# Gathering a token's two expert rows one per attention head over 64 heads, instead of two per head over the first 32

## What is computed

```python
# attention: two softmax maps for each head, and their difference
a1 = softmax(q1 @ k1.T * scale) @ v;  a2 = softmax(q2 @ k2.T * scale) @ v
o = rms_norm(a1 - lam * a2, sub_norm_w) * (1 - LAMBDA_INIT)
attn = o @ w_proj.T + b_proj
# experts: each token has two slots f1, f2 in the experts' rows eo, and two gates
eo = gelu(disp @ w_gate) @ w_down                     # (8 experts x 1024 slots, 256)
ffn = (g1 * keep1)[:, None] * eo[f1] + (g2 * keep2)[:, None] * eo[f2]
out = x + attn + ffn
```

## Time and profile before

| | |
|---|---|
| runs | 1810.17, 1812.2, 1918.32 us |
| profiled execution | 1807.14 us, span 1805.3 us |
| mean granted TensorE clock | 0.991 of full speed |
| TensorE busy | 1722.3 us (95%) |
| VectorE busy | 1486.1 us (82%) |
| ScalarE busy | 1402.3 us (78%) |
| GpSimd busy | 578.0 us (32%) |
| indirect gathers of expert rows | 64, 64.4 us on GpSimd, mean 1006 ns |

### The profile page before, as it was taken

How to read it: one execution, slowest core, us unless ns; L and a number is a source line. 1 busy time by engine, 2 the same in 40 slices (tenths; PEclk the granted TensorE clock), 3 DMA queues, 4 the chain that set the end, 5 groups by cost and what they waited for, 6 DMA issues and landing times.

```text
span 1805.3 us, 39337 instructions
## 1 busy us (share of the span) xinstructions
PE 1722.3 (95%) x15555; PEld 749.3 (42%) x15555; DVE 1486.1 (82%) x1727; ACT 1402.3 (78%) x2639; POOL 578.0 (32%) x1065
## 2 busy tenths in 40 slices
PE   6869999999999999999999999999999999999998
PEld 5437888888885222222222222222222222222226
DVE  7767777777767899898998999999999999999913
ACT  4535454445435999999999999999999999999993
POOL 1474221222200345445454454532121211112140
PEclk9989999999999999999999999999999999999999
DMA  7564233122203111111111111110101010100002
GB/s 239 197 216 148 93 108 94 59 71 88 89 12 117 35 44 36 49 34 40 45 37 48 35 41 43 38 41 23 32 23 32 23 29 27 27 11 5 5 1 94
DMA packets 92280, 109.66 MB, mean 61 GB/s; under 512 B 17472, under 2 KB 67264, under 8 KB 92096
## 3 DMA queue, kind: packets, MB, share of 16 engines
q1 hardware_dynamic: 85952, 90.36, 16.0%
q0 software_dynamic: 6144, 16.79, 3.2%
HBM read 72.77 MB, written 33.82 MB: 59 GB/s over the span
## 4 chain that ended last, share of the span: by engine, by line
PE 66%; ACT 27%; POOL 3%; DVE 2%; issue 1%; DMA 1%; ACTq 0%; SPq 0%; DVEq 0%; POOLq 0%
ACT arena_t L780 25%; PE banks L1223 18%; PE banks L1211 12%; PE banks L1262 10%; PE banks L1242 10%; PE banks L1193 8%; POOL arena_v L558 2%; PE banks L1282 2%; ACT o_raw L759 2%; PE banks L1116 2%; PE banks L1344 2%; PE banks L1162 1%; PE banks L1127 0%; DMA arena_x<-x_in 0%; DVE row_half L993 0%
## 5 line engine op out<-in xcount | busy, mean ns | idle before, releaser
L993 DVE TENSOR_REDUCE row_half<-banks 128x2 f32<-128x1024 f32 x1024 | 1189.7, 1218 | 144.7 <-PE banks L1193 136.5
L780 ACT ACTIVATE arena_t<-banks 128x512 f32<-128x512 f32 x2048 | 1085.2, 600 | 57.7 <-PE banks L1211 30.9
L1223 PE MATMUL banks<-arena_t,v_ring 128*17 128x256 f32 x8192 | 643.6, 386 | 26.2 <-ACT o_raw L759 26.1
L1223 PEld LDWEIGHTS banks<-arena_t,v_ring 128*17 128x17 f32 x8192 | 136.2, 95 | 403.4 <-issue 244.2
L1211 PE MATMUL banks<-arena_q 50*128 50x512 bf16 x960 | 286.2, 383 | 0.6 <-ACT arena_t L780 0.3
L1211 PE MATMUL banks<-qk_ring 50*128 50x512 bf16 x896 | 267.1, 387 | 7.1 <-ACT arena_t L780 4.1
L1193 PE MATMUL banks<-arena_q 48*128 48x512 bf16 x960 | 268.4, 384 | 0.5 <-DVE row_half L993 0.2
L1193 PE MATMUL banks<-qk_ring 48*128 48x512 bf16 x896 | 249.1, 382 | 1.1 <-DVEq L986 1.0
L744 ACT ACTIVATE arena_t<-banks 128x512 f32<-128x512 f32 x128 | 76.5, 598 | 205.8 <-PE banks L1242 197.1
L1262 PE MATMUL banks<-w_parts,hidden_parts 128*128 128x256 f32 x1536 | 196.3, 286 | 0.0
L1262 PEld LDWEIGHTS banks<-w_parts,hidden_parts 128*128 128x128 f32 x1536 | 187.1, 192 | 13.6 <-issue 13.6
(11 more groups left out here) (147 smaller groups left out, 1355.0 us busy)
## 6 DMA issues: line engine op xcount, KB each, us to landing
expert_rows<-arena_r SPq DMA_DIRECT2D x16, 512.0 KB, 3.0
q_stack<-arena_q SPq DMA_DIRECT2D x8, 768.0 KB, 4.9
k_stack<-arena_q SPq DMA_DIRECT2D x8, 768.0 KB, 3.5
v_heads<-arena_v SPq DMA_DIRECT2D x4, 1088.0 KB, 5.6
v_ring<-v_heads SPq DMA_DIRECT2D x64, 68.0 KB, 3.0
arena_x<-x_in SPq DMA_DIRECT2D x4, 1024.0 KB, 6.3
token_rows<-arena_x SPq DMA_DIRECT2D x4, 1024.0 KB, 7.8
arena_v<-w_gate_in SPq DMA_DIRECT2D x4, 1024.0 KB, 6.7
```

Of the source, the lines that this page charges most:

```text
L780: nc.scalar.activation(probs[:, kt % PSLOTS, q, :], banks[:, ST_BANKS[ring_place(i) % 3], :], ACT.Exp).then_inc(exp_done, 1)
L993: nc.vector.tensor_reduce(halves[:, :, j // 2], banks[:, SMAX_PAIRS[m % 2]:SMAX_PAIRS[m % 2] + 2, :], AX.X, ALU.max, negate=True).then_inc ...
L1223: mm = pe.matmul(banks[QUAD * q:QUAD * q + VP, OT_BANK, columns], v_ring[:, g % SLOTS, kt, :], probs[:, kt % PSLOTS, q, columns], start=(k ...
```

## The change

`gather` takes the choice c (0 or 1) as an argument and issues one indirect DMA instead of two. The tile and the choice are now counted from the head: head g issues the gather c = g mod 2 of tile t = g div 2. Even heads first combine the tile before and add the bias of tile t. Odd heads only gather. The last `combine` stands behind the loop over the heads, since tile 31's second gather is issued in head 63.

```diff
-            def gather(t):
-                if t == 0:
+            def gather(t, c):
+                if t == 0 and c == 0:
                     for s in range(2):
                         pool.wait_ge(rows_stored[s], 16 * E)
                 if t >= 2:
                     pool.wait_ge(acc_ready, 2 * (t - 1))
-                for c in range(2):
-                    nc.gpsimd.indirect_dma_start(
-                        out=gathered[:, t % 2, c, :], out_offset=None, in_=expert_rows,
-                        in_offset=bass.IndirectOffsetOnAxis(ap=slot_i[:, c, t:t + 1], axis=0)).then_inc(gather_in[t % 2], 16)
+                nc.gpsimd.indirect_dma_start(
+                    out=gathered[:, t % 2, c, :], out_offset=None, in_=expert_rows,
+                    in_offset=bass.IndirectOffsetOnAxis(ap=slot_i[:, c, t:t + 1], axis=0)).then_inc(gather_in[t % 2], 16)
...
                 scale_heads(g)
                 square_sums(g)
-                if 1 <= g <= NT:
-                    combine(g - 1)
-                if g < NT:
-                    add_bias(g)
-                    gather(g)
+                t, c = divmod(g, 2)
+                if c == 0:
+                    if t > 0:
+                        combine(t - 1)
+                    add_bias(t)
+                gather(t, c)
                 if g == NORM_FIRST_AT - 1:
                     for b in range(B - 1):
                         pool.wait_ge(inv_ready_first, 1)
                         normalize_heads(nc.gpsimd, b).then_inc(normed, 1)
+            combine(NT - 1)
```

## The result

The changed kernel took 1794.54 us (median of 4 runs, 1794.24 to 1796.11) against 1813.18 us for the kernel before on the same chip: ratio 0.9906, 95% interval 0.989 to 0.9921. The median of the kernel before takes in one slow run of 1918.32 us; its three others have a median of 1812.2 us, and the ratio goes by these.

A forecast was written before the change was run, and what follows sets the result against it. ScalarE was taken to bound the attention stage, losing 14.2 us to 32 pairs of gathers; lone gathers would cost 4.5 + 3.2 + 0.5 = 8.2 us instead, 6.0 less, so 1812.2 - 6.0 = 1806 us, range 1797 to 1817.

The forecast's parts named there:

- Where the loss is: Attention's first half: 32 gather pairs make ScalarE wait for score tiles, 14.2 us in all; multiplications and additions cost nothing.
- What is delayed: Attention stage: indirect DMAs delay TensorE while GpSimd works on them, 0.22 us for each gather if spread evenly.
- The gather of an even head: A lone gather 1.2 us behind the copy costs 0.42 us in one of three even heads, 4.5 us in all.
- The gather of an odd head: A lone gather 3 us before the copy costs 0.1 us in each of 32 odd heads, 3.2 us in all.
- The end: Closing stage: normalizations fit, last `combine` has some 25 us in hand; a lone gather may delay TensorE, 0.5 us.
- neg_split: Even heads: it queues behind 8.9 us of GpSimd work instead of 10.3; the transpose waiting for it stays unidled, cost 0.
- The scale: Whole kernel: runs' median stands 5 us above the profiled execution, so the forecast starts from 1812.2 us, not 1807.1.
- Rival 1: Attention stage: each gather delays TensorE by the same 0.22 us anywhere, 14.2 us as before, 1812 us; chance 0.24.
- rival 2: Both halves of attention: a lone gather costs what a pair does, 0.43 us; 13 us slower, 1825 us; chance 0.15.
- Rival 3: Attention stage: a lone gather fits into the slack, all 14.2 us are won, 1798 us; chance 0.13.
- Rival 4: First half of the heads: something other than the gathers delays TensorE and stays there, 1812 us; chance 0.04.
- Rival 5: Kernel's end: the last `combine` comes too late, which needs over 25 us of delay; chance 0.01.

The follow-up runs named there:

- no_gather: The changed kernel with all 64 gathers left out, so the experts' part is missing from the output; 1795.08 us, ratio 0.9921.
- split_in_head: The kernel before with each head's first gather ahead of `combine` and the second behind `add_bias`, still in heads 0 to 31; 1793.7 us, ratio 0.992.

## Why the prediction was wrong

*Where the loss is.* Right. The pairs cost ScalarE its exponentials in the first half, the multiplications and additions of `combine` cost none, and with lone gathers the heads take 18.23 and 18.41 us in turn, but for a few.

*What is delayed.* That "the indirect DMAs delay TensorE" was wrong. TensorE's multiplications start on time, and its semaphore updates come up to 0.99 us late; TensorE falls behind only after ScalarE, by the ring. The list of waits says that ScalarE waited for TensorE, and that is true of either case.

*The gather of an even head, 4.5 us.* This is the step that failed. The measured price is nothing (568.5 us against 568.4 without any gather, and ten exponentials in a row behind a lone gather in this place). I took the waits of 0.47 to 0.68 us for the first gather's, since the tile was due 0.3 us after the second gather's start and that seemed too short a time for the second to matter. They take both gathers. The update behind that wait was due 1.81 us behind the first gather's start and came 0.53 us late, and none that is due so far behind a lone gather is late. The trace before had no lone gather in this place to set the one against the other.

*The gather of an odd head, 3.2 us.* Also nothing. The nearest row did show that, eight exponentials at the usual pace behind the first gather of the first pair; I took 0.1 us each beside it with no row for them.

*The end, 0.5 us.* The last combine had 28 us in hand, the normalizations 1.1 us, as worked out. The cost of 0.5 isn't seen apart.

*`neg_split`.* Right: the transpose that waits for it stayed at 0.0 us idle (now L1009).

*The scale.* 14.2 us was worked out from one execution and carried over to the median by a fixed shift of 5 us. From profiled execution to profiled execution 12.9 us were won, a little less than 14.2. The medians of the first comparison lie 18.6 us apart (17.7 against 1812.2), since the profiled execution stands 0.3 us under the median in the changed kernel and 5 us under it in the kernel before. In the later comparisons the kernels without loss lie 14 to 18 us under the kernel before. So the full gain was near 14.2 in size, and the shift of the scale made up the rest; why the first median stood 5 us above its profile is not known. The kernel before spreads by 5 us from execution to execution also on the chip without the loss (1790.9 to 1796.17), so the spread is not the pairs'.

*The rivals.* Rival 1 (the price goes by the gather) and rival 2 (by the visit) are both refuted by `no_gather` and `split_in_head`. Rival 3, that a lone gather fits into the slack, had 0.13 and was right: its late updates, up to 0.41 us, are there in the trace after and cost nothing. Its 1798 was 3.5 us too high by the scale. Rival 4 (something else of the first half) is refuted by `split_in_head`, which keeps everything else in the first half. Rival 5, the late end, is refuted by the rows of the last `combine`. The chances as given add up to 1.01.

*The rule on ports.* The Trainium skill says that TensorE and ScalarE never wait on anyone for their memory ports ("SBUF — State Buffer", section "Who interferes with whom"). I took this for a forecast of no change, and as a forecast of time it failed in four comparisons; on one chip, at 1793.9 us before the change, the time is as it would have it. The traces don't speak against the rule itself: the multiplications start on time, and what is late is a semaphore update, of which that section says nothing.

## What to carry to other kernels

Indirect DMAs that GpSimd issues one right behind the other can hold up TensorE's semaphore updates by up to 1 us, and so slow engines that have nothing to do with them, if those hand work to each other with little in hand. Put 2 us of GpSimd's other work between them (here the `combine` that was there anyway), rather than leaving them side by side or spreading them thin. When a loss is put down to a pair of events, ask for a row with one of the two alone before giving each its share. When one engine waits for another, see whether the other started late or only its update came late. And before a loss of under 1% is taken for the kernel's own, see whether it is there on another chip.

## What the runs showed of the hardware

Three things were not expected. First, the loss goes with the chip: 1793.9 us on one, 1809.2 to 1813.2 us in four comparisons elsewhere, for the same kernel, with the granted clock at 0.99 in both kinds, and with no late update on the first. No chip is known to have served in two comparisons, so the chip and the occasion are not told apart. Second, the loss does not go by the bytes (a sixteenth: no less), nor does it fall with the rows (half: more), and 2.2 us between the starts end it. Third, it did not show among the experts' half steps. Here are two of the kernel before, one with four indirect gathers in direct succession and one without any, by busy time in the same execution as the earlier trace rows, and those gathers on GpSimd:

```profile
409.56:435.84 26.28, 26.28 (x170) 21.77 (x169) 19.21 (x23) 12.52 (x19) 6.99 (x6) 1.00 0.39 121
488.42:514.71 26.29, 26.29 (x170) 21.77 (x169) 19.06 (x21) 12.52 (x19) 0.00 (x0) 1.00 0.07 22
```

```profile
421.10 0.98 POOL L544 DMA_INDIRECT arena_r<-token_rows,token_i  x1 [6.55 <-PE banks L1162]
422.38 0.95 POOL L544 DMA_INDIRECT arena_r<-token_rows,token_i  x1 [0.30 <-issue]
423.63 0.95 POOL L544 DMA_INDIRECT arena_r<-token_rows,token_i  x1 [0.30 <-issue]
424.89 2.97 POOL L544 DMA_INDIRECT arena_r<-token_rows,token_i  x1 [0.30 <-issue]
```

Both half steps take 26.3 us with TensorE busy throughout, so its multiplications are not slowed there. For late updates they are no test: between 420.8 and 426.9 us TensorE had none to send. What holds the updates up, and why one chip is free of it, was not found.
